# Expert rows gathered as 16-bit halves, and results scattered by GpSimd to rows of choice and token

## What is computed

```python
x = x + attention(layernorm(x), wq, wk, wv, wo)          # causal, 32 heads over 8 key heads of 16
flat = layernorm(x)                                       # 2048 tokens
logits = flat @ router_w                                  # 64 experts
scores = softmax(logits)
_, topk_idx = top_k(logits + router_bias, 4)
topk_scores = scores at topk_idx, divided by their sum
routed = sum over the 4 chosen e of topk_score * (silu(flat @ wg[e]) * (flat @ wu[e])) @ wd[e]
shared = sum over 2 shared experts of (silu(flat @ swg) * (flat @ swu)) @ swd
x = x + routed + shared
```

## Time and profile before

| | us |
|---|---|
| median of 3 runs | 1158.7 |
| the runs | 1157.71, 1158.7, 1162.43 |
| the profiled execution, its own time | 1163.25 |
| its span, first to last instruction | 1161.4 |
| PE busy | 1090.9 (94%) |
| DVE busy | 818.3 (70%) |
| ACT busy | 571.3 (49%) |
| POOL busy | 458.5 (39%) |

### The profile page before, as it was taken

How to read it: one execution, slowest core, us unless ns; L and a number is a source line. 1 busy time by engine, 2 the same in 40 slices (tenths; PEclk the granted TensorE clock), 3 DMA queues, 4 the chain that set the end, 5 groups by cost and what they waited for, 6 DMA issues and landing times.

```text
span 1161.4 us, 29336 instructions
## 1 busy us (share of the span) xinstructions
PE 1090.9 (94%) x9641; PEld 493.2 (42%) x9641; DVE 818.3 (70%) x1324; ACT 571.3 (49%) x1123; POOL 458.5 (39%) x591
## 2 busy tenths in 40 slices
PE   5995899999999998899999999999999999998998
PEld 3533233333333332455444544544454444543443
DVE  6674899999999994697889345555555554537474
ACT  3311689889889889335303244444444433411010
POOL 5741233344344334205819533333333322227570
PEclk9997899999999999999999999999999999999999
DMA  8176032242232130342000488879887788647561
GB/s 244 40 184 150 19 68 43 49 75 41 44 79 41 42 62 3 135 156 74 1 1 1 162 262 285 240 228 319 246 270 212 217 313 283 192 121 237 177 189 65
DMA packets 76313, 161.67 MB, mean 139 GB/s; under 512 B 18644, under 2 KB 20052, under 8 KB 76260
## 3 DMA queue, kind: packets, MB, share of 16 engines
q1 hardware_dynamic: 42036, 92.72, 27.5%
q0 software_dynamic: 17216, 41.47, 12.4%
q10 hardware_dynamic: 17008, 26.76, 7.8%
HBM read 223.90 MB, written 41.42 MB: 228 GB/s over the span
## 4 chain that ended last, share of the span: by engine, by line
PE 54%; DVE 17%; issue 10%; DMA 7%; ACT 4%; POOL 3%; ACTq 2%; SPq 1%; DVEq 0%; POOLq 0%
PE PS L1423 10%; PE PS L1300 9%; PE PS L1405 7%; DVE maxes L1495 6%; DMA slot_y<-w_att 6%; PE PS L1214 5%; PE PS L1440 5%; PE PS L1095 4%; DVE max_low L1495 4%; PE PS L1163 3%; PE PS L1192 3%; ACTq L1052 2%; ACT att L956 2%; PE PS L1267 2%; PE PS L1383 2%
## 5 line engine op out<-in xcount | busy, mean ns | idle before, releaser
L956 ACT ACTIVATE att<-PS 128x512 f32<-128x512 f32 x576 | 312.5, 595 | 42.7 <-PE PS L1192 35.9
L1214 PE MATMUL PS<-att,v_head 128*32 128x256 f32 (+1 forms) x2560 | 178.7, 370 | 0.9 <-POOL att L761 0.9
L1495 DVE TENSOR_REDUCE maxes<-PS 128x2 f32<-128x1024 f32 (+2 forms) x192 | 172.8, 940 | 3.2 <-PE PS L1100 3.1
L1300 PE MATMUL PS<-XN,att 128*128 128x512 f16 x768 | 167.7, 379 | 4.9 <-DVE w_att L1744 3.7
L1495 DVE TENSOR_REDUCE max_low<-PS 128x2 f32<-128x1024 f32 x128 | 153.3, 1209 | 13.0 <-PE PS L1095 11.1
L875 POOL DMA_INDIRECT w_att<-xn_rows,idx x96 | 98.7, 1028 | 83.0 <-POOL idx L873 78.3
L1095 PE MATMUL PS<-att 48*128 48x512 f16 (+7 forms) x768 | 116.8, 328 | 15.5 <-DMA att<-ring 7.8
L1771 DVE SCALAR_TENSOR_TENSOR XT<-w_att,XT 128x512 f16<-128x512 f32 x96 | 66.4, 692 | 89.9 <-ACT XT L1030 89.9
L761 POOL TENSOR_SCALAR_AFFINE_SELECT att<-att 128x512 f32<-128x512 f32 (+1 forms) x96 | 74.9, 787 | 136.1 <-ACT att L956 135.3
L1192 PE MATMUL PS<-att 50*128 50x512 f16 (+1 forms) x640 | 112.3, 364 | 15.4 <-ACT att L956 13.1
L1036 ACT ACTIVATE w_att<-PS 128x512 f32<-128x512 f32 x96 | 57.3, 597 | 123.2 <-PE PS L1384 49.1
(11 more groups left out here) (188 smaller groups left out, 1625.1 us busy)
## 6 DMA issues: line engine op xcount, KB each, us to landing
ring<-in_L_ffn_wg_dram SPq DMA_DIRECT2D x96, 512.0 KB
XT<-in_L_ffn_wg_dram SPq DMA_DIRECT2D x96, 512.0 KB
ring<-in_L_ffn_wd_dram SPq DMA_DIRECT2D x96, 256.0 KB
XT<-in_L_ffn_wd_dram SPq DMA_DIRECT2D x96, 256.0 KB
slot_y<-w_att ACTq DMA_DIRECT2D x192, 128.0 KB
att<-q_stacks SPq DMA_DIRECT2D x60, 192.0 KB, 3.9
att<-k_stacks SPq DMA_DIRECT2D x60, 96.0 KB, 4.2
xn_rows<-w_att SPq DMA_DIRECT2D x16, 256.0 KB, 2.3
```

The lines of the kernel that those rows point to most:

```text
L956: act.activation(probs[:, n0 % RING, u * BANK:(u + 1) * BANK], bank((2 * n0 + u) % EXP_BANKS), ACT.Exp, scale=HD ** -0.5 / QK_SCALE ** 2). ...
L1214: mm = pe.matmul(PS[32 * r:32 * r + 32, at:at + qn], v_head[b][:, kt, :], probs[:, (NS * b + s) % RING, a:a + qn], start=s in (0, NS0), st ...
L1300: mm = pe.matmul(bank(2 * (n % 2) + k), shared_w[:, 2 * k + w, C * s + c, at:at + P], v[:, c, tokens], start=(c == 0 and w == 0 and v is x ...
L1495: last = dve.reduce_max(out, src, AXX)
```

## The change

Three parts go together.

1. **Halves in memory.** The second layer norm now scales its result by 16 (through the square root's `scale` and `eps_scaled`). For each tile ACT makes the high half in row form and POOL subtracts to get the low half; both go into `row_parts`, and SP writes these rows of 2 x 512 16-bit numbers to `xn2_rows`. The experts' gather fetches both halves at once, so PE turns `xg` directly; `tokens_high` and `tokens_low` of the expert stage are gone, and ACT copies the slot numbers into `idx`.
2. **Table with the choice.** The numbers that the routing table sums are plus or minus (1024 + token within its batch) times a power of two of the choice, so that DVE reads token and choice out of the bits of the sum, in eight small steps in place of one. A second table, `tab_y`, holds the row (batch, choice, token).
3. **Results scattered.** `choice_y` has a row for each choice and token. POOL writes each result there with one indirect DMA of 128 rows (empty slots are skipped), in place of ACT's two DMAs. The tail's loads are plain DMAs by SP, one for the four rows of each token of a tile, in place of POOL's 64 gathers.

```diff
-        xn2_rows = nc.dram_tensor("xn2_rows", [NTOK, D], FP32)
-        slot_y = nc.dram_tensor("slot_y", [SLOTS, D], FP32)
+        xn2_rows = nc.dram_tensor("xn2_rows", [NTOK, 2 * D], F16)
+        choice_y = nc.dram_tensor("choice_y", [TOPK * NTOK, D], FP32)
...
             for t in range(NT):
-                sp.wait_ge(xn2_ready, t + 1)
-                sp.dma_start(xn2_rows[t * P:(t + 1) * P, :], xn2[:, t % 4, :]).then_inc(xn2_stored, 16)
-                if t % 4 == 3:
+                if t % 4 == 1:
                     load_stage(2 + t // 4)
+                sp.wait_ge(row_lo_done, t + 1)
+                sp.dma_start(xn2_rows[t * P:(t + 1) * P, :], row_parts[:, t % 4, :]).then_inc(xn2_stored, 16)
...
+            def load_choices(t):
+                sp.dma_start(yk[:, t % YK, :, :], choices[t // (NT // 2), t % (NT // 2)]).then_inc(yk_in[t % YK], 16)
+
+            for done in yb_stored:
+                sp.wait_ge(done, 16 * PAIRS // 2)
+            for t in range(YK):
+                load_choices(t)
             for t in range(NT):
                 sp.wait_ge(mixed, TOPK * (t + 1))
+                if t + YK < NT:
+                    load_choices(t + YK)
...
+            def row_low(t):
+                pool.wait_ge(row_hi_done, t + 1)
+                pool.tensor_tensor(row_parts[:, t % 4, D:2 * D], xn2[:, t % 4, :], row_parts[:, t % 4, 0:D], ALU.subtract)\
+                    .then_inc(row_lo_done, 1)
+
+            for t in range(NT - 4):
+                row_low(t)
             swd_scale(0)
             swd_scale(1)
+            for t in range(NT - 4, NT):
+                row_low(t)
...
             def gather_tokens(i, j):
                 n = JP * i + j
 
-                wait(pool, xg_lo_done, n - 3)
-                pool.tensor_copy(idx[:, j:j + 1], tab_t[:, bass.ds(j * LANE_TILES + i, 1)]).then_inc(idx_set, 1)
                 wait_alone(pool, idx_set, n + 1, pool_passed)
...
+            def scatter_y(i, j):
+                n = JP * i + j
+                pool.wait_ge(idx_y_set, n + 1)
+                wait_alone(pool, yb_ready, n + 1, pool_passed)
+                pool.indirect_dma_start(out=choice_y[:, :],
+                                        out_offset=bass.IndirectOffsetOnAxis(ap=idx_y[:, j % 2:j % 2 + 1], axis=0),
+                                        in_=yb[:, j % 2, :], in_offset=None, bounds_check=TOPK * NTOK - 1,
+                                        oob_is_err=False).then_inc(yb_stored[j % 2], 16)
...
-            for j in range(JP):
-                gather_tokens(0, j)
-            with pool.Fori(1, LANE_TILES) as i:
+            for i in range(2):
                 for j in range(JP):
                     gather_tokens(i, j)
-
-            for s in yb_stored:
-                pool.wait_ge(s, 16 * PAIRS)
-            for t in range(NT):
-                if t >= YK:
-                    pool.wait_ge(mixed, TOPK * (t - YK + 1))
-                for k in range(TOPK):
-                    pool.indirect_dma_start(out=yk[:, t % YK, k, :], out_offset=None, in_=slot_y[:, :],
-                                            in_offset=bass.IndirectOffsetOnAxis(ap=slot_u[:, k, t:t + 1], axis=0))\
-                        .then_inc(yk_in[t % YK], 16)
+            with pool.Fori(2, LANE_TILES) as i:
+                for j in range(JP):
+                    gather_tokens(i, j)
+                    scatter_y(i - 2, j)
...
                     act.activation(x_hi[:, :, t * P:(t + 1) * P], bank(4 + t % 2).rearrange("p (c t) -> p c t", c=C),
-                                   ACT.Copy, scale=X_SCALE).then_inc(x_hi_ready, 1)
+                                   ACT.Copy).then_inc(x_hi_ready, 1)
+                    if t == 4 * g and g:
+                        act.wait_ge(xn2_stored, 64 * g)
+                    act.activation(row_parts[:, t % 4, 0:D], xn2[:, t % 4, :], ACT.Copy).then_inc(row_hi_done, 1)
...
             def turn_slots(n, k, i):
-                pe.wait_ge(xg_lo_done, n + 1)
+                pe.wait_ge(xg_in[k % JP], 16 * (i + k // JP + 1))
...
-                    dve.wait_ge(xn2_stored, 64 * g)
+                    dve.wait_ge(row_lo_done, 4 * g)
...
-            dve.tensor_scalar(tab_t[:, :], bank(6, PAIRS), float(NTOK), None, ALU.add).then_inc(table_ready, 1)
+            dve.tensor_copy(table_bits[:, :].bitcast(FP32), bank(6, PAIRS)).then_inc(table_step, 1)
...
-            def expert_y(n, j, count):
+            def expert_y(n, j, i, count):
+
+                wait(dve, yb_stored[j % 2], 16 * count)
+                dve.tensor_copy(idx_y[:, j % 2:j % 2 + 1], tab_y[:, bass.ds(j * LANE_TILES + i, 1)]).then_inc(idx_y_set, 1)
                 dve.wait_ge(e_down, n + 1)
-
-                wait(dve, yb_stored[j % 2], 32 * count)
                 dve.tensor_copy(yb[:, j % 2, :], bank(4 + j % 2)).then_inc(yb_ready, 1)
```

More of the change, by code:

```diff
@@ L822, in _ @@
                 .then_inc(consts, 1)
-            pool.tensor_scalar(token_f[:, :], token_f[:, :].bitcast(U32), float(-NTOK), None, ALU.add)\
-                .then_inc(consts, 1)
+            pool.tensor_copy(token_code[:, 1, :], token_code[:, 0, :].bitcast(U32)).then_inc(consts, 1)
             pool.tensor_copy(iota_t[:, :, :], iota_t[:, :, :].bitcast(U32)).then_inc(consts, 1)
             pool.wait_ge(consts, 15)
+            for k in (0, 2, 3, 1):
+                for h in range(2):
+                    half = slice(h * NT // 2, (h + 1) * NT // 2)
+                    pool.tensor_scalar(token_code[:, k, half], token_code[:, 1, half], (1 - 2 * h) * 2.0 ** (k - 1), None,
+                                       ALU.mult).then_inc(codes_set, 1)
             pool.affine_select(out=tile_no[:, LANES:], in_=tile_no[:, LANES:], compare_op=ALU.is_gt, fill=-1.0, base=0,
@@ L1046, in e_high, with next_tokens @@
                 act.activation(ht_hi[:, k % 2, :], ht[:, k % 2, :], ACT.Copy, scale=H_SCALE).then_inc(e_hidden_hi, 1)
-            def store_y(i, j):
-                act.wait_ge(yb_ready, JP * i + j + 1)
-                rows = slot_y.rearrange("(j l i q) d -> j l i q d", l=2, i=LANE_TILES, q=SUB)
-                for l in range(2):
-                    act.dma_start(rows[j, l, bass.ds(i, 1), :, :].rearrange("o q d -> (o q) d"),
-                                  yb[l * SUB:(l + 1) * SUB, j % 2, :]).then_inc(yb_stored[j % 2], 16)
+            def next_tokens(i, j):
+                act.activation(idx[:, j:j + 1], tab_t[:, bass.ds(j * LANE_TILES + i, 1)], ACT.Copy).then_inc(idx_set, 1)
             def expert_pairs(i, first, last):
@@ L1059, in expert_pairs @@
                         turned_tokens(n + 1, j + 1)
-                    if not (last and j >= JP - 2):
-                        tokens_high(n + 2, j + 2, i)
+                        if not last:
+                            next_tokens(i + 1 + (j + 1) // JP, (j + 1) % JP)
                     silu(n, j)
                     e_high(n, j)
-                    if not (first and j < 3):
-                        store_y(i if j == 3 else i - 1, (j + 1) % JP if j < 3 else 0)
-            for k in range(2):
-                tokens_high(k, k, 0)
+            act.wait_ge(table_ready, 1)
+            for j in range(JP):
+                next_tokens(0, j)
             turned_tokens(0, 0)
+            next_tokens(1, 0)
             expert_pairs(0, True, False)
@@ L1073, in _ @@
             expert_pairs(LANE_TILES - 1, False, True)
-            for j in range(1, JP):
-                store_y(LANE_TILES - 1, j)
             act.wait_ge(e_down, PAIRS)
@@ L1080, in _ @@
                 shared_silu(g)
-            for s in yb_stored:
-                act.wait_ge(s, 16 * PAIRS)
         @block.tensor
@@ L1395, in shared_down @@
                         pe.wait_ge(ident_h_set, 1)
[L1396 removed]
+                        turn_slots(0, 0, 0)
                     if t == 4 * EARLY:
@@ L1811, in expert_pairs @@
                     n = JP * i + j
-                    if not (last and j >= JP - 2):
-                        tokens_low(n + 2, j + 2)
                     expert_hidden(n, j)
```

81 lines of the change are left out of this document (50 added, 31 removed).

## The result

The changed kernel takes 1150.75 us (median of 6 runs, 1146.66 to 1153.62), the kernel before 1158.2 on the same chip (6 runs, 1156.35 to 1162.43): a ratio of 0.9921, 95% interval 0.9898 to 0.9943. In a later series of runs it was measured again: 1149.3 against 1159.9, ratio 0.9908 (0.9886 to 0.9929). So in these two series it is faster by 0.8 to 0.9%, 7.5 to 10.7 us, with an end of the first interval close to the half per cent that the prediction held to be the least that can be told apart. The forecast was 1154.0, in a range that holds the result. It gave "no change" the largest chance, 0.45; 1150.75 lies on the faster side of its limit of 1152.9.

What follows compares the result with a forecast made beforehand. PE was taken as the bound, with 10.8 us idle in the expert stage. Terms -6.3 + 1.3 - 2.0 = -7.0 us; two thirds, -4.7, off the median of 1158.7 gave 1154.0 us, range 1147 to 1165.

Steps and rivals of the forecast that it cites:

- Expert stage, -6.3: Expert stage: PE's waits behind DVE's delayed copy mostly go, 9.3 us at most with 3 kept as lost; -9.3 to +4.
- My 4.5 us: Expert stage: assumed time for a scatter to land, the usual late store's 4.1 us and a little for the gather.
- The landing is no earlier than it was: Expert stage: a store has 2.6 us free before DVE's next copy needs its buffer, against 2.8 before.
- Rival 1: Expert stage: stores land late all the time, steps grow from a landing of 4.95 us on; about 1173 us, chance 0.14.
- Rival 2: Expert stage: POOL becomes the bound, its two indirect DMAs making a step 3.78 us; about 1157 us, chance 0.08.
- Rival 3: Expert stage: PE waits for weights where it waited for L1771, stage gains only 1 us; 1157 us, chance 0.15.
- Rival 4: Second layer norm: costs 4 to 6 us, DVE and POOL excluding each other; 1158 us, chance 0.08.
- Second layer norm, +1.3: Second layer norm: DVE waiting for POOL's low half costs 0.8 us, the later routing chain 0.5; 0 to +4.
- Table: Routing table: DVE's eight small steps delay the first gather about 2 us, covered by 1.8 us; costs nothing.
- Tail, -2.0: Tail: of PE's 3.7 us of waits for DVE, 2.0 go since three loads are always ahead; 0 to -3.7.
- the stall of 1.66 stays: Tail: PE's wait of 1.66 us for DVE remains, since first data come about 1042, against 1042.86.
- From the profiled sum to the median: Whole kernel: a median execution has fewer of the stalls, so two thirds of the gain, -4.7 us, are kept.

Runs made afterwards that it cites:

- experiment 1: Two kernels, each with one half of the change: new halves with ACT's old stores, 1168.0 us; new scatter with the old halves, 1166.7 us.
- experiment 2: Changed kernel, each copy of results waiting for the scatter just before it: 1280.5 us; or a small GpSimd fill delaying each scatter: 1165.97 us.
- halves only: Changed kernel with the scatter and the tail's plain loads undone, halves in memory kept: 1168.0 us, ratio 0.994 to the kernel before.
- the earlier loads: Down weights of pair 1 issued ahead of SyncE's wait: kernel before with it 1157.1 us (0.9984), changed kernel with it 1145.3 us (0.9867).
- the first experiments: Series with the two half-change kernels and the one waiting for each scatter; there the kernel before took 1173.6 us, the changed kernel 1175.1.
- Scatter only: Changed kernel with the halves in memory undone, table, scatter and the tail's plain loads kept: 1166.7 us, ratio 0.9922 to the kernel before.
- one result: Changed kernel in which DVE copies a result only when the scatter of the one just before has landed: 1280.5 us, a single run.
- scatter first: Changed kernel with GpSimd's scatter of an older result issued ahead of the gather: 1149.6 us, ratio 0.9918 to the kernel before.
- both orders: Changed kernel with pair 1's down weights ahead of SyncE's wait and the scatter ahead of the gather: 1146.5 us, ratio 0.9891.

## Why the prediction was right, and where it was not

- **Expert stage, -6.3.** Right in mechanism, in its steps and in what stands where: DVE's waits for stores stayed (70 us; "30 us or more"), none reached PE, the step stayed at 3.67. The steady steps gained 9.7 and 9.0 us in the two pairs of profiles, 9.3 on average and the upper end of the term: the 3 us that I kept as lost are not there, since single late landings up to 7.6 us from the start of the issue, 6.6 from its end, were swallowed. The first four steps took back part: 16 to 20 us against 15 to 17. This start, in no row of the prediction, is what kept the profiled gain of the whole stage at 5.0 (359.5 to 354.6) in the first pair of profiles and made it 9.9 in the second.
- **How a scatter lands.** My 4.5 us count from the end of GpSimd's issue. In the same terms half of the waited landings took over 3.9 us (4.9 less the 1.0 of the issue), and half of all at most 3.5, so the figure was too long by about a microsecond. Of the two halves of the argument, "a late store no longer matters" is shown by experiment 1. "The landing is no earlier than it was" is not shown by itself: DVE's waits for stores were 57 us before and 70 after, but 80 with ACT's stores beside the new halves, and 80 in another profile of the changed kernel.
- **Rival 1** did not come. Its price was built nearly right: the prediction counts L from the end of the issue, and in its terms the round of experiment 2 is 0.68 + 0.88 + 1.02 + 0.07 + L, about 2.65 + L where it had 2.4 + L. With two buffers each step then grows from a mean L of 4.7, not 4.95. What kept the rival away is that L was shorter. But the danger was real: 1.14 us more lateness cost 16 us. The Trainium skill's rule beside it ("DMA: Bandwidth & Descriptors", "SWDGE vs HWDGE vs iDMA": queues of GpSimd and of ACT take turns) has no run that bears it out or denies it: DVE waited 80.3 us in 60 waits with the stores on ACT's queue (halves only) and 70.2 and 80.2 in 58, in two profiles, with them on GpSimd's, behind a gather. **Rival 2**: the gap on GpSimd is 0.31, below the 0.5 that was taken from the tail. **Rival 3**: PE's waits for weights in the steady steps are 1.1 us in all, against 0.3 in the second profile of the kernel before. **Rival 4** did not come either, as the next point shows.
- **Second layer norm, +1.3.** The step that failed is the wait of DVE for GpSimd's last low half, put at 0.4 us per group: groups start 13.86 us apart (495.55, 509.41), where before they were 13.86 too (498.98, 512.84). Timeline of DVE and GpSimd in the changed kernel's third profile, at the same place as the earlier trace rows and, in the last two rows, at the last change of groups:

```profile
497.38 2.28 DVE L1664 SCALAR_TENSOR_TENSOR att<-ring,att 128x2048 f16<-128x2048 f32 x1
498.21 2.48 POOL L875 TENSOR_TENSOR ring<-w_att,ring 128x512 f16<-128x512 f32 x1 [2.75 <-ACT ring L1011]
501.41 1.16 POOL L875 TENSOR_TENSOR ring<-w_att,ring 128x512 f16<-128x512 f32 x1 [0.72 <-ACT ring L1011]
523.15 5.69 POOL L860 TENSOR_SCALAR ring<-ring 128x1024 f32<-128x1024 f32 x2
523.28 4.10 DVE L1660 TENSOR_SCALAR w_att<-X,mv,rstd 128x512 f32<-128x512 f32 x4
```

  The subtraction takes 1.16 us alone and 2.48 when it starts inside DVE's L1664, and L1664 keeps its 2.28: the one that starts second waits, and here that is GpSimd, whose low half nobody waits for at that time. The Trainium skill's page "SBUF — State Buffer", section "SBUF: two separate sides", gives the port pair to whichever starts first for the whole instruction. The trace agrees (498.21 + 2.48 is 1.03 after the end of L1664), and the order of starting is what I had left out when I priced the rule at 1.2 us per group. Where GpSimd starts first DVE does pay: its last group takes 4.10 us beside GpSimd's scaling (L860), 2.63 before, when the scaling had begun earlier; PE didn't notice. Here the trace differs from that section of the Trainium skill: DVE's four instructions run inside the two of GpSimd, slowed to at most 1.36 us each from 0.54, and not held to the end of GpSimd's. What did come is 1.04 us before the second matmul groups of the shared expert, of which the prediction had 1.0 as the late silu. It went into PE's wait for the routing chain (the ranks), 1.61 and now 0.38. The 0.5 us by which that chain itself was to be later did not come: it let PE go on 63.6 us after A before and 63.4 now. Net -0.2, and +0.9 in the profiles in which the clock dips once there (0.92 between 540 and 562 us in the first profile).
- **Table.** Nothing, as forecast: PE did not wait for the first tile.
- **Tail, -2.0.** Measured -4.2. The failed step is "the stall of 1.66 stays": PE's waits for DVE in the tail, 3.7 us before, are gone (0.2 in the third profile). My own sum had the first data 0.9 us earlier, and I still kept the whole stall. The last scatter also landed sooner than I put it (timeline of the changed kernel where the earlier trace rows had the gathers):

```profile
1027.80 0.98 POOL L914 DMA_INDIRECT choice_y<-w_att,idx_y  x1 [1.94 <-DVE w_att L1842]
1029.95 2.32 SPq L663 DMA_DIRECT2D ring<-choice_y  x3
1035.76 1.54 DVE L1870 SCALAR_TENSOR_TENSOR X<-ring,small,X 128x512 f32<-128x512 f32 x2 [4.78 <-DMA ring<-choice_y]
```

  The scatter lands 1.2 us after GpSimd is done with it. PE's tail begins at 1024.08, so the first adding comes 11.7 us into it; before, 13.6 (1042.86 against 1029.28). 1.9 us are more than the stall of 1.66.
- **From the profiled sum to the median.** The sum was -7.0, and I kept two thirds of it, since a median execution would have fewer of the stalls. That is the weakest step: two profiles of the kernel before, at 1162.4 and 1163.3 us, and one of it with the earlier loads, at 1154.2, all have 7.4 to 8.5 us of waits for L1771. Half of the 9.1 us between the longest and the shortest lies in the first 500 us, not in what the change removes. With all of the -7.0 the forecast had been 1151.7, within a microsecond of the 1150.75 and on the faster side of the limit. That the -7.0 itself lies so near the measured -7.45 is partly luck: the steady steps and the tail gave some 5 us more than their terms, and in the first pair of profiles the start of the expert stage took 4.7 us of it back.

## What to carry to other kernels

Look for what stands behind a delayed instruction on its engine before working on the delay: here DVE waits 57 to 80 us for stores in either version, and it cost PE 8 us only while the next thing in DVE's queue was one that PE needed soon. Say from which end of an issue a landing is counted (the two differ by 1.0 us here), and don't discount a stall as chance unless a second profile lacks it. At a stage's start, loads whose memory is already free should not queue behind a wait for other memory: moving the down weights of one pair ahead gave the changed kernel 4 us, about half as much as the whole change.

## What was unexpected

In the series of the first experiments the kernel before took 1173.6 us (26 runs, 1168 to 1180) and the changed kernel 1175.1 (10 runs), a ratio of 1.0013 (0.9986 to 1.0041): no gain at all, where the two other series with both kernels show 0.8 to 0.9%.

> The changed kernel once more, for a second profile on this chip. The start of the expert stage had one wait of 3.0 us (fourth step, weights of lanes 6 and 7) and a stretch at the lower clock, together 5.8 us over undisturbed steps. If the wait is built in (the last weights of the first round are issued only when the shared expert's down projection has ended, at 666.9, and 4 MB land in a burst), it comes again within 1 us of the same size; if it is chance, it is absent or elsewhere. Time 1146 to 1154.

From the eleventh step on ACT starts a silu 2 to 3 us late in about every second step; 38 such waits, 147 us in all, have a releaser that the profile doesn't name. ACT's wait in that profile, and the timeline of PE and ACT in one such step:

```profile
ACT w_att L1073 <- remote: 147.4, 38, 4.8
```

```profile
739.59 1.95 PE L1447 MATMUL PS<-ring,w_att 128*64 128x256 f32 x16
740.67 0.19 ACT L1081 ACTIVATE idx<-small 128x1 uint32 x1
743.26 2.12 PE L1447 MATMUL PS<-ring,w_att 128*64 128x256 f32 x16
744.68 0.28 ACT L1073 ACTIVATE w_att<-PS 128x128 f32<-128x128 f32 x1 [3.82 <-remote]
746.18 0.27 ACT L1073 ACTIVATE w_att<-PS 128x128 f32<-128x128 f32 x1
```

PE's group ends at 741.54, and nothing else that this silu waits for in the program is open, yet it starts at 744.68; the next one, whose group ends at 745.38, starts as soon as ACT's queue comes to it. PE loses 0.8 to 1.0 us by each of those looked at, and the steady steps are 28 us longer than in the other profiles of the same kernel. Scatter only had two such waits in that series, one result none, and halves only none in the expert stage but three, 26 us, in the tail, where PE stood 8.5 us (its 147.1 in the table). It is not simply that chip: its number on record is 15, and with the same number the kernel before took 1159.4 us in a later series (that of scatter first and both orders). Whether it belongs to how the programs were loaded that time I did not try, and the kernel before was not profiled there. So the gain of the change holds for two of three series, and why it was absent in the third stays open.

The clock: in the changed kernel's first profile a wait of 3.03 us was followed by a group at 3.68 us, at a granted clock of 0.50, the lower of the two levels. In its second profile a longer wait at the same place was not:

```profile
674.00 1.95 PE L1447 MATMUL PS<-XT,w_att 128*64 128x256 f32 x16 [3.07 <-issue]
```

The same program thus differs by some 3 us at one place from one execution to the next, and the length of the wait alone does not say whether the clock falls.
